# Attention on one Trainium2 core: the next step's scores issued one head per quarter of a step

## The chip, the cores and the metric

The kernel runs on one NeuronCore of one Trainium2 chip. The metric is the device time of one execution in microseconds (us): 3027.41 before the change, the median of three runs (3024.32 to 3032.85).

Names used below: PE is TensorE, DVE is VectorE, ACT is ScalarE, POOL is GpSimd, and SP is the engine that here issues the loads and stores. PSUM is the memory that PE writes; one of its eight banks holds 512 float32 values in each of the 128 partitions.

## What is computed

A block of mixture-of-experts, attention, mixture-of-experts, each with a residual:

```python
x = x + 0.5 * ffn(layernorm(x))      # 8 experts, one per token, capacity 1024
x = x + attention(layernorm(x))
x = x + 0.5 * ffn(layernorm(x))
```

with x of 8 batches x 1024 tokens x 256, float32. The change concerns the attention alone, which has 16 heads of 16 columns:

```python
q, k, v = heads(Wq, bq), heads(Wk, bk), heads(Wv, bv)
q, k = rope(q), rope(k)
att = einsum('bhqd,bhkd->bhqk', q, k) / sqrt(16)      # causal
att = softmax(where(causal, att, -1e10))
y = einsum('bhqk,bhkd->bhqd', att, v)
return y @ Wp.T + bp
```

## The kernel before, in words

The program is a row of blocks: routing, experts, attention, routing (with attention's last projection), experts. In the profile the attention takes about 815 to 2230 us of the span.

**Groups and steps.** Attention works through 32 *groups*; a group is four heads of one batch. A group has 12 *steps* (`STEPS`, L50): in a step the four heads' scores are computed of one block of 128 keys against up to 512 queries (half a batch). Steps 0 to 3 belong to the first half of the queries, steps 4 to 11 to the second. A step on the diagonal has fewer columns (steps 1, 2, 3 and 5, 6, 7 have 128, 256 and 384) and a second matmul that adds the mask (L1440). So four kinds of work run in each step:

- *Scores* (`scores`, L1428): per head one matmul, and on the diagonal the mask matmul, into one of `BANKS` = 3 PSUM banks, `score_ps`. A head's score waits on `exp_done` until the exponential that read that bank three heads earlier is done.
- *Exponentials* (`exponentials`, L1318) on ACT, one per head, from `score_ps` to `probs`. ACT also copies the finished half `o_ps` (L1316), and splits the rotated q and k of a later pair of token tiles into parts (`first_parts` L1306, `second_parts` L1311) in steps 1, 3 and 5.
- *Times V* (`times_v`, L1443): four heads side by side in the array, from `probs` to `o_ps`. It waits until all four exponentials of its own step are done, and in steps 0 and 4 for ACT's copy of `o_ps`.
- The *ring* (`ring`, L1415 on PE, L1179 on DVE): for the group after, PE computes scores again, queries by keys, into one of three banks `max_ps`, and DVE takes each row's maximum. 48 such matmuls per group, and two transposes of the finished maxima (`FIRST` and `SECOND`, L1419), are dealt out over the 12 steps and within a step over its four *quarters* c = 0 to 3 (`share`, L113). A ring matmul waits until DVE has read its bank three places earlier. The maxima are subtracted inside the score matmul: they go as three more rows into q. For that DVE splits them into three bfloat16 parts (`split_peaks`, L1208), PE transposes these, DVE copies them to `peak_t`, and SP writes them to memory and reads them back into q (`move_peaks`, L982 to L990). The scores of steps 0 and 4 wait for this second transfer (`peak_loaded`, L1433).

**Preparation.** In between, each group prepares two more token tiles, six groups ahead (`piece`, L1502): PE transposes rotated q and k in steps 0 and 3, normalized x in step 5, and multiplies by the weights in steps 6, 8 and 10; all go through the one bank `prep_ps`, which DVE (`leave` L1173, `xt_low` L1153, `add_bias_qk` L1159) and ACT read. POOL rotates (`rope`, L1053) and makes the third part (`third_parts`, L1078). SP then stores the pair (`store_pair`, L954), loads q, k and v of the group after next (`load_group`, L967: 13 transfers), and only then does it move the next group's maxima of the first half (`move_peaks(..., 0)`). These waits and transfers stand in one queue, that of SP. From group 27 on nothing is left to prepare.

**The order within a step.** It is written out by hand in `body` of the PE program (L1488). Before the change a quarter is: piece, then in quarters 0 and 1 the scores of two heads of the step after, then in quarter 2 times V of this step, then the ring's share. The scores of the next group's step 0 are issued in step 11. That point, the first score matmul of a group, is called the *group's start* below.

Of the kernel before, what the change touches and what calls it, by code (L numbers as in the profile page):

```python
# [22 lines left out]
P = 128  # L23
# [15 lines left out]
GH = 4  # L39
# [9 lines left out]
BANKS = 3  # L49
STEPS = [(0, j) for j in (0, 3, 2, 1)] + [(1, j) for j in (0, 7, 6, 5, 4, 1, 2, 3)]  # L50
NS = len(STEPS)
HALF = S // 2
# [763 lines left out]
def attention_block(nc, sh, dr):  # L816
# [6 lines left out]
    with ExitStack() as ctx:  # L823
# [9 lines left out]
        q = [sb(f"q{k}", [ROWS_M, GH, S], BF16) for k in range(SLOTS)]  # L833
        kk = [sb(f"k{k}", [ROWS_M, GH, S], BF16) for k in range(SLOTS)]
# [70 lines left out]
        score_ready = sem("score_ready")  # L905
# [29 lines left out]
        def slot_round(g, k, ahead):  # L935

            if isinstance(g, int):
                return (g + ahead) % SLOTS, (g + ahead) // SLOTS
            return (k + ahead) % SLOTS, g // SLOTS + (k + ahead) // SLOTS
# [423 lines left out]
        def _(pe):  # L1363
# [61 lines left out]
                te.matmul(max_ps[bank(u, r)][:, 0:w], q[u][0:ROWS, h, i * P:(i + 1) * P], kk[u][0:ROWS, h, k0:k0 + w],  # L1425
                          start=True, stop=True).then_inc(max_ready, 1)

            def scores(g, u, t, pr):  # L1428

                c0, w, diagonal = columns(STEPS[t])  # L1430
                hf, j = STEPS[t]
                if t in FIRST_STEP.values() and pr == 0:
                    pe.wait_ge(peak_loaded[hf], 16 * (g + 1))  # L1433
                for h in range(2 * pr, 2 * pr + 2):
                    pe.wait_ge(exp_done, GH * (NS * g + t) + h + 1)
                    out = score_ps[(GH * t + h) % BANKS]
                    last = te.matmul(out[:, 0:w], kk[u][:, h, j * P:(j + 1) * P],  # L1437
                                     q[u][:, h, hf * HALF + c0:hf * HALF + c0 + w], start=True, stop=not diagonal)
                    if diagonal:
                        last = te.matmul(out[:, 0:P], sh.ident_bf[:], hide_bf[:], start=False, stop=True)  # L1440
                    last.then_inc(score_ready, 1)

            def times_v(g, u, t):  # L1443
                c0, w, _ = columns(STEPS[t])
# [37 lines left out]
            pe.wait_ge(qkv_loaded[1], 16 * LOADS)  # L1482
            for r in RING_STEPS[NS - 1]:
                ring(1, 1, r)
            for pr in range(2):
                scores(0, 0, 0, pr)

            def body(g, k, more, prepare, finish):  # L1488
                n = g + LEAD
                for t in range(NS):  # L1490
# [29 lines left out]
                                product_v(n, s)  # L1520

                    for c in range(SHARES):
                        piece(c)
                        if c < 2:
                            if t + 1 < NS:
                                scores(g, k, t + 1, c)
                            elif more:
                                scores(g + 1, slot_round(g, k, 1)[0], 0, c)
                        if c == 2:
                            times_v(g, k, t)  # L1530
                        places(c)
# [101 lines left out]
```

## Time and profile before

| | before |
|---|---|
| median of three runs | 3027.41 us (3024.32 to 3032.85) |
| the profiled execution | 3024.25 us, with a span of 3022.4 us |
| PE busy | 2263.0 us (75% of the span), 14405 matmuls |
| weight loads busy | 1441.9 us (48%) |
| DVE busy | 1717.5 us (57%) |
| ACT busy | 1193.7 us (39%) |
| POOL busy | 961.9 us (32%) |
| mean granted TensorE clock | 0.898 of full speed |
| scores, 1536 matmuls (L1437) | 448.7 us, 337 ns each |
| mask, 1024 matmuls (L1440) | 219.4 us, 226 ns each |
| exponentials, 1536 (L1324) | 648.4 us, 495 ns each |

How to read it: busy is the time in which at least one instruction of the engine was under way. PE's matmuls overlap: a row lists the time from a matmul's start to its modelled end, and the next may start before that end. So two starts, one after the other, tell better what a matmul costs PE than its duration does, and an idle time listed before a matmul is shorter than the wait was. The clock is the share of full speed that the chip granted to TensorE: 1.00 is 2.4 GHz, 0.5 is 1.2 GHz, and a value between is a mean over a stretch in which both occurred. In a timeline the columns are start, duration (both us), engine, line, operation, written tile and read tiles, shape and count, and in brackets the engine's idle time before it with what ended it; "issue" there means nothing that the profile can name on another engine, such as a DMA.

### The profile page before, as it was taken

What the parts mean: (1) busy time and instruction counts of PE and PEld (TensorE: products, weight loads), DVE (VectorE), ACT (ScalarE), POOL (GpSimd) and SP (SyncE); (2) the same over time, 40 slices, a digit from 0 to 9 for tenths busy, and PEclk for the clock granted to TensorE, in tenths of its full rate; (3) what the DMA queues carried; (4) which work ended last, traced back from release to release, by engine and by line L of the source; (5) the groups of instructions that cost most, each with busy time, mean ns of one, the idle gap of its engine ahead of it and who ended that gap; (6) DMA issues with size and microseconds to landing.
All of it is one profiled execution on the core that took longest, in us unless ns stands there. A gap on an engine that the chain in (4) does not pass through costs nothing. (4 is left out here: it accounts for less than half of the span.)

```text
span 3022.4 us, 43677 instructions
## 1 busy us (share of the span) xinstructions
PE 2263.0 (75%) x14405; PEld 1441.9 (48%) x14405; DVE 1717.5 (57%) x5075; ACT 1193.7 (39%) x2498; POOL 961.9 (32%) x1308
## 2 busy tenths in 40 slices
PE   2704999974488888888888888888945550499997
PEld 2704888863333333333333333332315550488887
DVE  3503555534277776777677676776726660355553
ACT  1202444431135555555555555555631120244443
POOL 1173444324513232222222223320013427344442
PEclk9999999995579999999999999999976665699999
DMA  8026323202534455446355445534322202622320
GB/s 339 0 99 209 100 72 100 70 22 84 122 64 92 90 103 98 95 88 117 78 100 103 89 80 99 99 75 87 68 80 90 83 1 95 213 99 69 99 73 20
DMA packets 227444, 284.52 MB, mean 94 GB/s; under 512 B 21303, under 2 KB 171704, under 8 KB 225184
## 3 DMA queue, kind: packets, MB, share of 16 engines
q1 hardware_dynamic: 214944, 248.68, 33.3%
q0 software_dynamic: 12288, 33.21, 3.1%
q8 instruction: 110, 1.80, 0.3%
q14 instruction: 102, 0.84, 0.1%
HBM read 154.78 MB, written 127.66 MB: 93 GB/s over the span
## 5 line engine op out<-in xcount | busy, mean ns | idle before, releaser
L1324 ACT ACTIVATE at_probs<-at_score_ps 128x512 f32<-128x512 f32 (+3 forms) x1536 | 648.4, 495 | 521.6 <-PE at_score_ps L1440 379.0
L1203 DVE CUSTOM_DVE_ANT_0 at_junk<-at_max_ps,at_causal 128x128 f32<-128x128 f32 (+3 forms) x1024 | 490.5, 485 | 233.2 <-PE at_max_ps L1425 227.7
L1437 PE MATMUL at_score_ps<-at_q,at_k 99*128 99x512 bf16 (+3 forms) x1536 | 448.7, 337 | 89.9 <-ACT at_probs L1324 50.1
L1425 PE MATMUL at_max_ps<-at_k,at_q 96*128 96x512 bf16 (+3 forms) x1536 | 455.5, 342 | 9.9 <-DVE at_peak L1206 6.3
L1206 DVE TENSOR_REDUCE at_peak<-at_max_ps 128x1 f32<-128x512 f32 x512 | 352.1, 688 | 152.1 <-PE at_max_ps L1425 150.2
L728 DVE TENSOR_TENSOR f_hid_lo<-f_hid,f_hid_hi 128x512 fp32r<-128x512 f32 x256 | 177.5, 693 | 311.2 <-ACT f_hid_hi L752 310.8
L1450 PE MATMUL at_o_ps<-at_probs,at_v 128*32 128x512 f32 (+3 forms) x3072 | 340.9, 517 | 0.1
L790 PE MATMUL f_y_ps<-f_w_hi,f_hid_hi 128*128 128x256 f32 x1024 | 292.9, 286 | 40.4 <-DVE f_xe L709 28.9
L749 ACT ACTIVATE f_hid<-f_hid_ps 128x512 f32<-128x512 f32 x256 | 153.1, 598 | 418.1 <-PE f_hid_ps L775 393.0
L1425 PEld LDWEIGHTS at_max_ps<-at_k,at_q 96*128 96x128 bf16 x1536 | 129.6, 99 | 348.8 <-DVE at_peak L1203 144.7
L790 PE MATMUL f_y_ps<-f_w_hi,f_hid_lo 128*128 128x256 f32 x1024 | 291.5, 285 | 0.0
L790 PE MATMUL f_y_ps<-f_w_lo,f_hid_hi 128*128 128x256 f32 x1024 | 290.2, 283 | 0.0
L1437 PEld LDWEIGHTS at_score_ps<-at_q,at_k 99*128 99x128 bf16 x1536 | 143.7, 99 | 262.5 <-ACT at_probs L1324 152.9
L1064 POOL TENSOR_TENSOR at_by_cos<-at_qk,at_cos 128x512 f32<-128x512 f32 x64 | 81.4, 1272 | 534.2 <-DVE at_qk L1162 534.2
L653 POOL TENSOR_SCALAR f_xn<-f_xe 128x256 f32<-128x256 f32 x128 | 175.1, 1375 | 214.0 <-PE f_xt_ps L763 134.7
L790 PEld LDWEIGHTS f_y_ps<-f_w_hi,f_hid_hi 128*128 128x128 f32 x1024 | 194.3, 190 | 63.4 <-issue 41.2
L1440 PE MATMUL at_score_ps<-at_hide_bf,ident_bf 128*128 128x128 bf16 x1024 | 219.4, 226 | 0.0
L763 PE MATMUL f_xt_ps<-ident,f_xn 128*128 128x128 f32 x256 | 39.9, 282 | 217.1 <-POOL f_xn L653 217.1
L790 PEld LDWEIGHTS f_y_ps<-f_w_lo,f_hid_hi 128*128 128x128 f32 x1024 | 194.2, 190 | 9.0
L790 PEld LDWEIGHTS f_y_ps<-f_w_hi,f_hid_lo 128*128 128x128 f32 x1024 | 194.1, 190 | 0.0
L1080 POOL TENSOR_TENSOR at_part<-at_rest,at_part 128x512 bf16<-128x512 f32 x64 | 74.0, 1156 | 341.9 <-ACT at_part L1311 341.9
L775 PE MATMUL f_hid_ps<-f_xt_hi,f_w_hi 128*128 128x512 f32 x512 | 167.8, 409 | 14.9 <-DVE f_w_lo L691 14.9
(140 smaller groups left out, 3843.6 us busy)
## 6 DMA issues: line engine op xcount, KB each, us to landing
f_w_raw<-in_w SPq DMA_DIRECT2D x32, 1024.0 KB, 7.5
qk<-at_part SPq DMA_DIRECT2D x96, 256.0 KB, 2.9
at_q<-qk SPq DMA_DIRECT2D x192, 128.0 KB, 4.9
at_k<-qk SPq DMA_DIRECT2D x192, 128.0 KB, 7.7
expert_in<-zeros SPq DMA_DIRECT2D x16, 1040.0 KB, 25.6
f_xe<-expert_in SPq DMA_DIRECT2D x32, 520.0 KB, 3.7
v_rows<-at_v_out SPq DMA_DIRECT2D x64, 256.0 KB, 3.6
at_v<-v_rows SPq DMA_DIRECT2D x32, 512.0 KB, 9.6
```

What stands on the lines that cost most here:

```text
L653: last = nc.gpsimd.tensor_scalar(xn[:, t, :], x[:, t, 0:C], x[:, t, MEAN:MEAN + 1], x[:, t, RSTD:RSTD + 1], ALU.subtract, ALU.mult)
L728: v.tensor_tensor(hid_lo[f % NHID][:], hid[f % NHID][:], hid_hi[f % NHID][:].bitcast(F32), ALU.subtract).then_inc(hid_lo_ready, 1)
L749: nc.scalar.activation(hid[f % NHID][:], hid_ps[f % 2][:], ACT.Gelu_apprx_tanh).then_inc(hid_ready, 1)
L775: last = nc.tensor.matmul(hid_ps[f % 2][:], w[ws][:, cc, f * P:(f + 1) * P], x[b % 2][:, cc, :], start=(i == 0), stop=(i == 3 * CC - 1))
L790: last = nc.tensor.matmul(y_ps[t][:], a[m][:, rows], w[ws][:, f, :], start=(f == 0 and i == 0), stop=(f == FC - 1 and i == 2))
L1203: v.tensor_tensor_reduce(junk[bank(k, r)][:, 0:w], src, causal[:, HALF - w:HALF], 1.0, LEAST, ALU.add, ALU.max, out).then_inc(max_used, 1)
L1206: v.tensor_reduce(out, src, AX.X, ALU.max).then_inc(max_used, 1)
L1324: a.activation(probs[t % 2][:, h, c0:c0 + w], score_ps[(GH * t + h) % BANKS][:, 0:w], ACT.Exp, scale=float(SCALE)).then_inc(exp_done, 1)
L1425: te.matmul(max_ps[bank(u, r)][:, 0:w], q[u][0:ROWS, h, i * P:(i + 1) * P], kk[u][0:ROWS, h, k0:k0 + w], start=True, stop=True).then_inc(m ...
L1437: last = te.matmul(out[:, 0:w], kk[u][:, h, j * P:(j + 1) * P], q[u][:, h, hf * HALF + c0:hf * HALF + c0 + w], start=True, stop=not diagonal)
L1440: last = te.matmul(out[:, 0:P], sh.ident_bf[:], hide_bf[:], start=False, stop=True)
L1450: last = te.matmul(o_ps[h * VW:(h + 1) * VW, c0:c0 + w], vv[u][:, j, h, :], probs[t % 2][:, h, c0:c0 + w], start=(t == FIRST_STEP[hf]), st ...
```

## The change

`scores` now takes one head instead of a pair. In each of the four quarters of a step it is called first, ahead of piece, times V and the ring's share. The four heads' scores of the step after so stand at the start of quarters 0, 1, 2 and 3, where two stood in each of quarters 0 and 1, behind the piece.

```diff
-            def scores(g, u, t, pr):
+            def scores(g, u, t, h):
...
-                if t in FIRST_STEP.values() and pr == 0:
+                if t in FIRST_STEP.values() and h == 0:
                     pe.wait_ge(peak_loaded[hf], 16 * (g + 1))
-                for h in range(2 * pr, 2 * pr + 2):
-                    pe.wait_ge(exp_done, GH * (NS * g + t) + h + 1)
...
+                pe.wait_ge(exp_done, GH * (NS * g + t) + h + 1)
...
                     for c in range(SHARES):
+                        if t + 1 < NS:
+                            scores(g, k, t + 1, c)
+                        elif more:
+                            scores(g + 1, slot_round(g, k, 1)[0], 0, c)
                         piece(c)
-                        if c < 2:
-                            if t + 1 < NS:
-                                scores(g, k, t + 1, c)
-                            elif more:
-                                scores(g + 1, slot_round(g, k, 1)[0], 0, c)
                         if c == 2:
                             times_v(g, k, t)
                         places(c)
```

The instructions are the same on every engine, and on DVE, ACT, POOL and SP their order is the same too. Only PE's order moves. (In the changed kernel L1437, L1440 and L1450 are L1436, L1439 and L1449.)

The first place is step 2 of a group on PE: the scores of step 3 (384 columns, with mask) and times V of step 2 (256 columns). Before:

```order
L1437 MATMUL at_score_ps<-at_q,at_k 128x384
L1440 MATMUL at_score_ps<-at_hide_bf,ident_bf 128x128
L1437 MATMUL at_score_ps<-at_q,at_k 128x384
L1440 MATMUL at_score_ps<-at_hide_bf,ident_bf 128x128
L1437 MATMUL at_score_ps<-at_q,at_k 128x384
L1440 MATMUL at_score_ps<-at_hide_bf,ident_bf 128x128
L1437 MATMUL at_score_ps<-at_q,at_k 128x384
L1440 MATMUL at_score_ps<-at_hide_bf,ident_bf 128x128
L1425 MATMUL at_max_ps<-at_k,at_q 128x512
L1450 MATMUL at_o_ps<-at_probs,at_v 32x256 x4
L1425 MATMUL at_max_ps<-at_k,at_q 128x512
```

Changed:

```order
L1436 MATMUL at_score_ps<-at_q,at_k 128x384
L1439 MATMUL at_score_ps<-at_hide_bf,ident_bf 128x128
L1436 MATMUL at_score_ps<-at_q,at_k 128x384
L1439 MATMUL at_score_ps<-at_hide_bf,ident_bf 128x128
L1425 MATMUL at_max_ps<-at_k,at_q 128x512
L1436 MATMUL at_score_ps<-at_q,at_k 128x384
L1439 MATMUL at_score_ps<-at_hide_bf,ident_bf 128x128
L1449 MATMUL at_o_ps<-at_probs,at_v 32x256 x4
L1436 MATMUL at_score_ps<-at_q,at_k 128x384
L1439 MATMUL at_score_ps<-at_hide_bf,ident_bf 128x128
L1425 MATMUL at_max_ps<-at_k,at_q 128x512
```

The first ring matmul moved ahead of the third score, and times V ahead of the fourth.

The second place is step 11 on PE, from the first mask matmul after the group's start to the transpose of the second half's maxima. Before:

```order
L1440 MATMUL at_score_ps<-at_hide_bf,ident_bf 128x128
L1437 MATMUL at_score_ps<-at_q,at_k 128x512
L1440 MATMUL at_score_ps<-at_hide_bf,ident_bf 128x128
L1425 MATMUL at_max_ps<-at_k,at_q 128x128 x2
L1437 MATMUL at_score_ps<-at_q,at_k 128x512
L1440 MATMUL at_score_ps<-at_hide_bf,ident_bf 128x128
L1437 MATMUL at_score_ps<-at_q,at_k 128x512
L1440 MATMUL at_score_ps<-at_hide_bf,ident_bf 128x128
L1425 MATMUL at_max_ps<-at_k,at_q 128x128 x2
L1450 MATMUL at_o_ps<-at_probs,at_v 32x512 x4
L1425 MATMUL at_max_ps<-at_k,at_q 128x256 x3
L1419 MATMUL at_max_ps<-ident_bf,at_peak_part 48x128
```

Changed:

```order
L1425 MATMUL at_max_ps<-at_k,at_q 128x128 x2
L1436 MATMUL at_score_ps<-at_q,at_k 128x512
L1439 MATMUL at_score_ps<-at_hide_bf,ident_bf 128x128
L1425 MATMUL at_max_ps<-at_k,at_q 128x128 x2
L1436 MATMUL at_score_ps<-at_q,at_k 128x512
L1439 MATMUL at_score_ps<-at_hide_bf,ident_bf 128x128
L1449 MATMUL at_o_ps<-at_probs,at_v 32x512 x4
L1425 MATMUL at_max_ps<-at_k,at_q 128x256 x2
L1436 MATMUL at_score_ps<-at_q,at_k 128x512
L1439 MATMUL at_score_ps<-at_hide_bf,ident_bf 128x128
L1425 MATMUL at_max_ps<-at_k,at_q 128x256
L1419 MATMUL at_max_ps<-ident_bf,at_peak_part 48x128
```

Each pair of ring matmuls stands one score earlier, and the first two 256-column ones now come after three scores instead of four.

The third place is step 3 on PE, where the scores are those of step 4 and the transposes of rotated q and k (L1410) are the piece. Before:

```order
L1410 MATMUL at_prep_ps<-ident,at_rot 128x128 x2
L1437 MATMUL at_score_ps<-at_q,at_k 128x512 x2
L1410 MATMUL at_prep_ps<-ident,at_rot 128x128 x2
L1437 MATMUL at_score_ps<-at_q,at_k 128x512 x2
L1425 MATMUL at_max_ps<-at_k,at_q 128x512
L1450 MATMUL at_o_ps<-at_probs,at_v 32x384 x4
L1425 MATMUL at_max_ps<-at_k,at_q 128x512
```

Changed:

```order
L1436 MATMUL at_score_ps<-at_q,at_k 128x512
L1410 MATMUL at_prep_ps<-ident,at_rot 128x128 x2
L1436 MATMUL at_score_ps<-at_q,at_k 128x512
L1410 MATMUL at_prep_ps<-ident,at_rot 128x128 x2
L1425 MATMUL at_max_ps<-at_k,at_q 128x512
L1436 MATMUL at_score_ps<-at_q,at_k 128x512
L1449 MATMUL at_o_ps<-at_probs,at_v 32x384 x4
L1436 MATMUL at_score_ps<-at_q,at_k 128x512
L1425 MATMUL at_max_ps<-at_k,at_q 128x512
```

The second transposes end after two scores in both orders; the ring matmul and times V stand ahead of the fourth score.

## Rows read from the trace of the kernel before

**Rows 1.** Busy time by stretch; one whole group, steady state.

```profile
core 0: us, PE busy (x) PEld busy (x) DVE busy (x) ACT busy (x) POOL busy (x), PEclk, DMA share, GB/s
1305.30:1349.74 44.44, 38.92 (x264) 16.80 (x263) 31.97 (x109) 24.00 (x55) 12.98 (x22) 0.96 0.45 91
```

**Rows 2.** Who waited for whom, PE, 945 to 2017 us (24 groups): total, times, longest.

```profile
PE at_score_ps L1437 <- ACT at_probs L1324: 37.3, 97, 1.0
PE at_max_ps L1419 <- DVE at_peak_part L1227: 31.2, 24, 1.8
PE at_score_ps L1437 <- issue: 23.9, 18, 2.5
```

**Rows 3.** Timeline around one group's start, SP and PE.

```profile
1323.18 1.52 SPq L960 DMA_DIRECT2D qk<-at_part  x3
...
1335.56 0.36 SPq L986 DMA_DIRECT2D peaks<-at_peak_t  x1
1344.56 0.72 SPq L989 DMA_DIRECT2D at_q<-peaks  x1
...
1346.94 0.38 PE L1437 MATMUL at_score_ps<-at_q,at_k 99*128 99x512 bf16 x1 [0.49 <-issue]
```

**Rows 4.** Busy time of first halves, group's start to store issue; columns of rows 1.

```profile
902.33:923.99 21.66, 18.67 (x138) 7.98 (x138) 15.10 (x65) 13.43 (x35) 6.61 (x8) 0.92 0.07 26
...
1302.49:1323.18 20.69, 17.25 (x138) 7.77 (x138) 15.36 (x67) 13.41 (x35) 6.61 (x7) 1.00 0.07 27
...
1702.73:1726.97 24.24, 21.34 (x146) 9.34 (x146) 15.19 (x66) 13.90 (x35) 6.79 (x8) 0.80 0.06 24
...
sum 552.02, PE 466.59 PEld 207.18 DVE 405.67 ACT 349.27 POOL 171.66; mean PE 17.95 PEld 7.97 DVE 15.60 ACT 13.43 POOL 6.60
```

**Rows 5.** The same for 25 second halves, store issue to next group's start.

```profile
1057.58:1079.81 22.23, 20.07 (x127) 8.47 (x126) 15.97 (x42) 10.55 (x22) 6.37 (x15) 1.00 0.84 156
...
1411.41:1435.61 24.20, 20.08 (x127) 8.49 (x126) 16.65 (x43) 10.54 (x22) 6.36 (x15) 1.00 0.82 143
...
sum 583.10, PE 518.17 PEld 219.06 DVE 402.75 ACT 263.77 POOL 156.75; mean PE 20.73 PEld 8.76 DVE 16.11 ACT 10.55 POOL 6.27
```

**Rows 6.** Timeline of PE, steps 1 and 3 of one group.

```profile
1310.34 0.22 PE L1440 MATMUL at_score_ps<-at_hide_bf,ident_bf 128*128 128x128 bf16 x1
1310.75 0.28 PE L1437 MATMUL at_score_ps<-at_q,at_k 99*128 99x256 bf16 x1 [0.20 <-ACT at_probs L1324]
1310.87 0.22 PE L1440 MATMUL at_score_ps<-at_hide_bf,ident_bf 128*128 128x128 bf16 x1
1310.93 0.33 PE L1425 MATMUL at_max_ps<-at_k,at_q 96*128 96x384 bf16 x1
...
1314.96 0.38 PE L1437 MATMUL at_score_ps<-at_q,at_k 99*128 99x512 bf16 x1
...
1316.30 0.39 PE L1437 MATMUL at_score_ps<-at_q,at_k 99*128 99x512 bf16 x1 [0.96 <-ACT at_probs L1324]
1316.53 0.38 PE L1425 MATMUL at_max_ps<-at_k,at_q 96*128 96x512 bf16 x1
```

**Rows 7.** Timeline of ACT, steps 3 and 4, the same group.

```profile
1315.16 0.58 ACT L1306 CAST at_part<-at_prep_ps 128x512 bf16<-128x512 f32 x1 [0.77 <-PE at_prep_ps L1410]
1315.64 2.07 ACT L1324 ACTIVATE at_probs<-at_score_ps 128x512 f32<-128x512 f32 x4
```

**Rows 8.** Timeline of PE, DVE and POOL, step 11.

```profile
1305.65 1.27 POOL L1064 TENSOR_TENSOR at_by_cos<-at_qk,at_cos 128x512 f32<-128x512 f32 x1 [11.89 <-DVE at_qk L1162]
...
1305.98 0.96 DVE L1227 TENSOR_TENSOR at_peak_part<-at_peak_rest,at_peak_part 128x16 bf16<-128x16 f32 x1
...
1307.09 0.22 PE L1419 MATMUL at_max_ps<-ident_bf,at_peak_part 128*48 128x128 bf16 x1 [1.43 <-DVE at_peak_part L1227]
```

**Rows 9.** Timeline of ACT and POOL, step 5.

```profile
1321.11 0.62 ACT L1311 CAST at_part<-at_rest 128x512 bf16<-128x512 f32 x1 [1.93 <-DVE at_rest L1176]
...
1321.80 1.15 POOL L1080 TENSOR_TENSOR at_part<-at_rest,at_part 128x512 bf16<-128x512 f32 x1 [6.17 <-ACT at_part L1311]
```

**Rows 10.** Who waited for whom, PE, 2069 to 2210 us (last groups).

```profile
PE at_score_ps L1437 <- ACT at_probs L1324: 5.3, 22, 0.4
```

More of the change, by code:

```diff
@@ L1426, in ring @@
                           start=True, stop=True).then_inc(max_ready, 1)
-            def scores(g, u, t, pr):
+            def scores(g, u, t, h):
                 c0, w, diagonal = columns(STEPS[t])
                 hf, j = STEPS[t]
-                if t in FIRST_STEP.values() and pr == 0:
+                if t in FIRST_STEP.values() and h == 0:
                     pe.wait_ge(peak_loaded[hf], 16 * (g + 1))
-                for h in range(2 * pr, 2 * pr + 2):
-                    pe.wait_ge(exp_done, GH * (NS * g + t) + h + 1)
[L1436 to L1441, printed above, removed]
+                pe.wait_ge(exp_done, GH * (NS * g + t) + h + 1)
+                out = score_ps[(GH * t + h) % BANKS]
+                last = te.matmul(out[:, 0:w], kk[u][:, h, j * P:(j + 1) * P],
+                                 q[u][:, h, hf * HALF + c0:hf * HALF + c0 + w], start=True, stop=not diagonal)
+                if diagonal:
+                    last = te.matmul(out[:, 0:P], sh.ident_bf[:], hide_bf[:], start=False, stop=True)
+                last.then_inc(score_ready, 1)
             def times_v(g, u, t):
@@ L1484, in _ @@
                 ring(1, 1, r)
-            for pr in range(2):
-                scores(0, 0, 0, pr)
+            for h in range(GH):
+                scores(0, 0, 0, h)
             def body(g, k, more, prepare, finish):
```

## The prediction, made before the changed kernel ran

> **What bounds the kernel now.** I read four views. First the busy time by stretch: in a steady group [rows 1] PE is busy 38.92 of 44.44 us, DVE 31.97, ACT 24.00. No engine is full, so what counts is who waits for whom. Second, the waits of PE over 24 groups [rows 2]: the scores wait for exponentials (37.3 us, 97 times, so four times a group), the transpose of the second half's maxima for DVE (31.2 us, once a group), and the scores wait 18 times for something that is on no engine (23.9 us). Third, the timeline around a group's start [rows 3]: that last wait ends 2.38 us after SP issued the read of the maxima into q at 1344.56. Their write had been issued at 1335.56 and waited 9 us among the 13 loads, which stand behind the store at 1323.18. So one chain is SP's: store, loads, maxima, group's start.
>
> Fourth, I cut each group in two: the first half from the group's start to the issue of the store, the second from there to the next start. Second halves [rows 5] last 22.2 to 24.2 us, on average 583.10 / 25 = 23.3, though PE needs only 20.1 us of each at full clock, and the DMA share is over 0.8. In 18 of 24 groups, then, the second half is as long as its transfers. First halves [rows 4] move almost nothing (DMA share 0.07). They last 20.69 us at full clock, and longer where the clock was lower: 21.66 at 0.92, 24.24 at 0.80. Their end is set by engines: DVE frees `prep_ps` (L1176), ACT splits at 1321.11, POOL at 1321.80 [rows 9], and the store follows.
>
> The reader is to see this: **what PE saves in a first half brings the store, and with it the whole period, forward. What it saves in a second half only makes the wait at the group's start longer.**
>
> **The change part by part.** No instruction is added or removed; each of 32 groups has its 48 scores in another place on PE.
>
> *The fourth head's score.* It needs the bank of the first head of its own step, so that exponential must be over; the other three wait for those of the step before. Where all four are issued within quarters 0 and 1, PE stands still for it. A mask matmul that is not held up is followed 0.06 us later by the next (1310.87, 1310.93); the one before the fourth head by 0.41 (1310.34, 1310.75), a wait of 0.35 us of which the row shows 0.20 as idle [rows 6]. The same sum gives 0.35 in step 2 and 0.13 in step 0. In step 3 it is 1316.30 less 1314.96, less 0.23 for a 512-column score: 1.1 us, because ACT first does its cast at 1315.16 and begins the exponentials at 1315.64 [rows 6, 7]. Now times V stands between. In step 1 it has 128 columns and is the shortest, in step 3 384. I walked the steps forward with these rows: the first exponential is over before times V is, except in step 3, where PE would reach the fourth score at about the time that the exponential begun at 1315.64 ends (about 0.6 us later: four take 2.07, overlapping), and some 0.2 us of waiting remain. The cast itself comes no earlier by the new order, since the second transposes stand behind two scores as before. First halves gain 0.13 + 0.35 + 0.35 + 0.9 = **1.75 us**. Bounds: nothing, if the next exponential is late in the same measure, and 1.95.
>
> *The maxima in step 11.* PE stands idle 1.43 us until DVE has made the last part [rows 8]. That instruction took 0.96 us though it has 16 columns, and ended as POOL's product of 1305.65 ended (1305.98 + 0.96 = 1306.94; 1305.65 + 1.27 = 1306.92). POOL's product waits for DVE's bias addition (L1162), which stands behind ring places issued in quarters 0 and 1. These now stand one score (0.28 us with its mask) or two earlier, and the wait of the fourth score in between is gone (0.24). So the bias addition, POOL's product and the last part all come about 0.6 us earlier. Gain **0.6 us**, between 0 and the whole 1.43 that would be free if DVE came ahead of POOL.
>
> *What follows in the first half.* Steps 4 and 5 hang on DVE: from the last ring place of step 3 to the release of `prep_ps` it works without a pause. It is moved forward as a whole by what PE gained until then. Two waits that PE newly meets in step 4 (for the second and third exponential, and for ACT's copy of `o_ps`) stand beside this DVE work, which is the longer; I cost them at nothing. If they were longer than DVE's work, up to 0.5 us a group would be lost. No engine becomes full: DVE's 15.4 us of a first half would fill 15.4 of 18.3.
>
> Sum of a first half: 1.75 + 0.6 = 2.35 us. There are 27 with such a store: **63 us**.
>
> *Second halves.* Similar waits go there too (steps 5, 7 and 9, and the earlier rings in step 5), about 1.3 us by the same arithmetic. Six or seven of 25 second halves ended without a wait at the start and have 0.3 to 0.5 us of room before their transfers bind: **3 us**. The rest only lengthens the wait at the group's start.
>
> *The last groups* have no store and few transfers, and are bound by PE and ACT. Scores wait 5.3 us in 22 places as idle time [rows 10], and each is 0.15 longer as in rows 6: 8.6 us. I take nearly all: **8 us**.
>
> *The clock.* After the longest waits at a group's start the granted clock is lower. Eight of 26 first halves are at 0.92 or less; all 26 sum to 552.02 us [rows 4], 14.1 over 26 x 20.69, so 1.7 us for each of the eight. Of the waits at a start, 2.5 us at most [rows 2], the seven longest are the ones followed by it. With 1.3 us added to each wait some 18 are as long as those seven are now, and I count 18 of 26 first halves in place of eight: ten more, **17 us lost**. Bounds: none more (0), all 26 (31).
>
> The Trainium skill, "TensorE: Matmul & The Clock Gate", section "HAM oscillation — how this bites in real kernels", says that a wait for a DMA between batches of matmuls takes the clock back to half, so that each batch starts cold, every time. This speaks against the change. The rows agree for the long waits and not for the short ones; by that rule the loss would be the upper bound, 31 us.
>
> Total: 63 + 3 + 8 - 17 = 57 us off the profiled execution's 3024.25, that is 2967. The median of the runs is 3.2 above that execution: **2970 us**.
>
> **The rivals.**
>
> *Every group starts cold.* For it: waits at the start grow in every group. Against: 1.3 us more leaves many below the length of the seven. 14 us slower than the forecast: 2984.
>
> *The wait only moves.* The three banks `score_ps` are as few as before. If the fourth exponential, asked for later, is late for quarter 2 of the next step, only the gain in step 11 is left: 27 x 0.6 = 16, so 3011. For it: the exponentials of 512 columns start every half microsecond, and a step of few columns has little PE work from quarter 3 to the next quarter 2. Against: ACT is busy 13.4 of 20.69 us in first halves [rows 4]. The Trainium skill, "Perfetto Trace Analysis", section "Optimization Strategy" (under "Identifying Performance Opportunities"), says that a gap that repeats can mean too few buffers in PSUM; by that reading an order alone gives little, and this rival's time is what it would give.
>
> *Second halves gain too*, if the transfers run faster once the engines do: 1.3 us in 25 halves, 32 us, and no more cold starts: 2921. Against: 150 GB/s whatever PE does [rows 5].
>
> *Slower.* In the new order the fourth score stands behind times V, and times V of the next step needs its exponential. If PE then waits a whole exponential (0.6 us) in each of a first half's six steps, that is 3.6 us against 2.35 gained: 1.25 x 27 = 34 us slower, 3061. It decides from 0.4 us a step on. Against: between a fourth score and the next times V stand three more scores and two or three ring matmuls, in wide steps over 1 us of PE work.
>
> *No change*: first halves gain, and the transfers' half grows by as much. Nothing in rows 5 speaks for it.
>
> **How the numbers follow.** Forecast 0.55 (2970); every group cold 0.14 (2984); the wait moves 0.14 (3011, or part of it); second halves too 0.09 (2921); slower 0.05 (3061); no change 0.03. A difference of 0.3%, 9 us, is about what the measurement can tell. Faster by more: 0.55 + 0.14 + 0.14 + 0.09 = 0.92. Slower by more: 0.05. Within: 0.03. For the range: the bounds of the forecast's own terms reach from full gain without more cold starts (1.95 + 0.8 per first half, 74 + 3 + 8 = 85 off, 2942) to half the gain of first halves with the middle clock loss (31 + 3 + 8 - 17 = 25 off, 3002). I take 2938 to 3004, which leaves out the third rival's end, part of the second and the last two.
>
> **What would show it.** Right: from step 0 to 3 no idle before the fourth head's score but some 0.2 us in step 3; the transpose of the maxima waits about 0.8 us, not 1.43; first halves at full clock of about 18.3 us; second halves as long as before (23.3); more and longer waits at the group's start; more first halves below full clock. Wrong: first halves of 20 us or more with waits of scores for exponentials in quarter 0 to 2; second halves clearly longer or shorter than 23.3; a period of 44 us as now.

## The result: 2.7% faster, and the profile after

| | before | changed |
|---|---|---|
| median of four runs | 3029.58 us (3024.32 to 3032.85) | 2945.26 us (2938.67 to 2954.99) |
| ratio, 95% interval | | 0.9732 [0.9714, 0.9751] |
| the profiled execution | 3024.25 us | 2954.99 us |
| PE / DVE / ACT busy, share of span | 75 / 57 / 39% | 75 / 58 / 41% |

The change saves 84 us by the medians. The profiled execution of the changed kernel is the longest of its four, that of before is shorter than all of its four, so the two traces show less: 3022.4 - 2953.2 = 69.2 us of span. The forecast was 57 off one profiled execution, 2970 us, in a range of 2938 to 3004. Time and sign were right; of the size, 57 us was forecast where the profiled executions show 69 and the medians 84. Among all executions named below one stands apart, 5038.8 us in the run "fourth score alone", whose median is therefore taken over its other three.

The page of the changed kernel begins:

```profile
span 2953.2 us, 43675 instructions
...
PE 2219.3 (75%) x14403; PEld 1436.2 (49%) x14405; DVE 1702.0 (58%) x5075; ACT 1222.7 (41%) x2498; POOL 962.5 (33%) x1308
```

The waits of PE, changed kernel, 937 to 1956 us (25 groups), beside [rows 2]:

```profile
PE at_score_ps L1436 <- issue: 64.6, 24, 4.4
...
PE at_max_ps L1419 <- DVE at_peak_part L1227: 14.9, 20, 1.1
PE at_max_ps L1425 <- DVE at_peak L1203: 12.2, 42, 0.5
```

The first line of [rows 2], 97 waits for exponentials, has no counterpart: there is none in this stretch. The wait for the last part of the maxima is halved (31.2 to 14.9 us). The wait at the group's start has nearly tripled, 23.9 to 64.6. That is the answer in three lines: one wait went, one was halved, and one took part of the room. The last line above is smaller: ring matmuls, which now stand earlier, wait for DVE 42 times in first halves, where before it was once (0.3 us). On the other hand, the preparation's transposes of x no longer wait for DVE's release of `prep_ps`, which before read

```profile
PE at_prep_ps L1371 <- DVE at_rest L1176: 8.4, 24, 0.4
```

The busy time by stretch of the changed kernel, first halves (columns as in [rows 1]); beside [rows 4]:

```profile
1101.46:1119.71 18.25, 16.96 (x145) 7.96 (x146) 15.26 (x66) 13.61 (x34) 6.61 (x7) 1.00 0.08 31
1144.59:1163.98 19.39, 18.45 (x145) 8.37 (x146) 15.16 (x66) 13.74 (x34) 6.61 (x7) 0.91 0.08 30
...
sum 497.76, PE 467.46 PEld 213.04 DVE 396.23 ACT 353.43 POOL 171.73; mean PE 17.98 PEld 8.19 DVE 15.24 ACT 13.59 POOL 6.61
```

and the second halves, here 26 where [rows 5] has 25 (the first one of before, 23.81 us, makes 606.9 of its 583.1):

```profile
1078.63:1101.46 22.83, 19.36 (x118) 8.37 (x117) 15.96 (x43) 11.30 (x22) 6.38 (x15) 1.00 0.84 151
...
sum 604.66, PE 504.78 PEld 217.81 DVE 414.33 ACT 293.59 POOL 163.36; mean PE 19.41 PEld 8.38 DVE 15.94 ACT 11.29 POOL 6.28
```

First halves took 552.0 us in all and now take 497.8: 54.3 less. Second halves took 606.9 and now take 604.7: 2.3 less, although PE is busy 20.70 - 19.41 = 1.3 us less in each on average, 0.74 of it at full clock (20.10 and 19.36). At full clock a first half is 18.25 us where it was 20.69.

Where the other 69.2 - 56.5 = 12.7 us came from: every 48th score matmul begins a group. The start of group 1 comes 5.9 us earlier (902.3 to 896.4), the stretch from group 27's start to group 31's is 9.0 us shorter (138.8 to 129.8), and what follows that is 1.2 us longer. Of the 5.9 us, 3.4 lie before group 0's start (857.22 to 853.84), ahead of any instruction whose place was changed; in the runs below with pairs prepared six ahead that start lies between 852.1 and 856.2 us, in either order. Group 0 itself gained 2.6 us (45.1 to 42.5). Its second half is the first of the 26 above, so 0.8 us stand in both counts.

The places themselves. Step 3 of a first half, timeline of PE in the changed kernel, beside [rows 6, 7]:

```profile
1112.94 0.85 PE L1449 MATMUL at_o_ps<-at_probs,at_v 128*32 128x384 f32 x8
1113.75 0.39 PE L1436 MATMUL at_score_ps<-at_q,at_k 99*128 99x512 bf16 x1
```

and of ACT in the same step:

```profile
1112.61 0.58 ACT L1306 CAST at_part<-at_prep_ps 128x512 bf16<-128x512 f32 x1
1113.09 2.07 ACT L1324 ACTIVATE at_probs<-at_score_ps 128x512 f32<-128x512 f32 x4
```

The fourth score at 1113.75 has no idle time before it: the exponential begun at 1113.09 ran beside times V and was over at 1113.70. Before, 1.1 us of standing still were here.

Step 11 of the same group, timeline of POOL, DVE and PE, beside [rows 8]; the group's start was 1101.46:

```profile
1104.00 1.26 POOL L1064 TENSOR_TENSOR at_by_cos<-at_qk,at_cos 128x512 f32<-128x512 f32 x1 [12.07 <-DVE at_qk L1162]
...
1104.75 0.54 DVE L1227 TENSOR_TENSOR at_peak_part<-at_peak_rest,at_peak_part 128x16 bf16<-128x16 f32 x1
...
1105.44 0.22 PE L1419 MATMUL at_max_ps<-ident_bf,at_peak_part 128*48 128x128 bf16 x1 [0.73 <-DVE at_peak_part L1227]
```

POOL's product starts 2.54 us after the group's start, where it was 3.16; PE's transpose follows at 3.98, where it was 4.60. DVE's 16-column instruction again ends when POOL's product ends (1105.29 and 1105.26).

SP's chain is as it was, 9 us from the write of the maxima to their read in [rows 3] and here, and the start comes 2.37 us after the read is issued. SP's queue in the changed kernel, before another start:

```profile
1133.15 0.36 SPq L986 DMA_DIRECT2D peaks<-at_peak_t  x1
1142.22 0.72 SPq L989 DMA_DIRECT2D at_q<-peaks  x1
```

and PE's first instruction at that start:

```profile
1144.59 0.40 PE L1436 MATMUL at_score_ps<-at_q,at_k 99*128 99x512 bf16 x1 [4.40 <-issue]
```

### The profile page after: what moved, and what is told of

The parts are those of the page before. It is cut to its first block and busy times, and to the rows that moved or that the text cites. A ratio compares the mean times of both kernels' runs of the same rounds, so it can differ in the third digit from the quotient of the medians.

```text
span 2953.2 us, 43675 instructions
## 1 busy us (share of the span) xinstructions
PE 2219.3 (75%) x14403; PEld 1436.2 (49%) x14405; DVE 1702.0 (58%) x5075; ACT 1222.7 (41%) x2498; POOL 962.5 (33%) x1308
## 5 line engine op out<-in xcount | busy, mean ns | idle before, releaser
L1324 ACT ACTIVATE at_probs<-at_score_ps 128x512 f32<-128x512 f32 (+3 forms) x1536 | 690.8, 498 | 512.3 <-PE at_score_ps L1439 371.4
L1436 PE MATMUL at_score_ps<-at_q,at_k 99*128 99x512 bf16 (+3 forms) x1536 | 503.7, 335 | 83.6 <-issue 79.7
L1425 PE MATMUL at_max_ps<-at_k,at_q 96*128 96x512 bf16 (+3 forms) x1536 | 489.4, 341 | 23.2 <-DVE at_peak L1203 14.9
L1449 PE MATMUL at_o_ps<-at_probs,at_v 128*32 128x512 f32 (+3 forms) x3072 | 342.5, 519 | 1.5 <-ACT at_o_out L1316 0.8
L1425 PEld LDWEIGHTS at_max_ps<-at_k,at_q 96*128 96x128 bf16 x1536 | 144.6, 99 | 378.0 <-DVE at_peak L1203 163.6
L1436 PEld LDWEIGHTS at_score_ps<-at_q,at_k 99*128 99x128 bf16 x1536 | 151.3, 99 | 202.1 <-issue 92.9
L1439 PE MATMUL at_score_ps<-at_hide_bf,ident_bf 128*128 128x128 bf16 x1024 | 227.3, 224 | 0.0
L790 PEld LDWEIGHTS f_y_ps<-f_w_hi,f_hid_hi 128*128 128x128 f32 x1024 | 194.3, 190 | 63.5 <-issue 41.7
L775 PE MATMUL f_hid_ps<-f_xt_hi,f_w_hi 128*128 128x512 f32 x512 | 167.5, 408 | 14.6 <-DVE f_w_lo L691 14.6
L700 DVE TENSOR_TENSOR f_xt_lo<-f_xt_ps,f_xt_hi 128x512 fp32r<-128x512 f32 x64 | 44.3, 692 | 229.7 <-ACT f_xt_hi L740 229.7
```

The source lines that it names most:

```text
L775: last = nc.tensor.matmul(hid_ps[f % 2][:], w[ws][:, cc, f * P:(f + 1) * P], x[b % 2][:, cc, :], start=(i == 0), stop=(i == 3 * CC - 1))
L790: last = nc.tensor.matmul(y_ps[t][:], a[m][:, rows], w[ws][:, f, :], start=(f == 0 and i == 0), stop=(f == FC - 1 and i == 2))
L1324: a.activation(probs[t % 2][:, h, c0:c0 + w], score_ps[(GH * t + h) % BANKS][:, 0:w], ACT.Exp, scale=float(SCALE)).then_inc(exp_done, 1)
L1449: last = te.matmul(o_ps[h * VW:(h + 1) * VW, c0:c0 + w], vv[u][:, j, h, :], probs[t % 2][:, h, c0:c0 + w], start=(t == FIRST_STEP[hf]), st ...
```

## The experiments

The theory (T): the gain is that of waits removed in first halves; second halves are as long as SP's transfers. Rivals: it comes from all twelve steps alike; or from the scores' place ahead of the pieces, not from the fourth one's place behind times V. Each run was compared with runs of the kernel before on the same chip; the medians of those were 3022.7 to 3033.0 us, so ratios compare better than times. The means are of the profiled executions: 26 halves in the runs with pairs six ahead, and for first halves 25 with pairs seven ahead. The kernel before has 21.23 and 23.34. With pairs seven ahead the last of the 26 second halves has nothing left to prepare (14.6 us in the new order, 15.6 in the old); without it the means are 20.52, 22.15 and 20.40 in the table's order. In the run with early maxima the store stands elsewhere, and the halves do not compare.

| run | median, us | ratio, 95% interval | first halves, mean | second halves, mean |
|---|---|---|---|---|
| changed kernel | 2945.3 | 0.9732 [0.9714, 0.9751] | 19.14 | 23.26 |
| new order in first halves only | 2948.5 | 0.9739 [0.9691, 0.9786] | 18.78 | 23.21 |
| new order in second halves only | 3033.2 | 1.0022 [0.9999, 1.0045] | 22.20 | 23.25 |
| fourth score alone | 2956.8 | 0.9757 [0.9693, 0.9821] | 19.44 | 23.23 |
| pairs ahead of pieces | 3044.3 | 1.0064 [1.0044, 1.0084] | 21.90 | 23.27 |
| new order in step 11 only | 3007.4 | 0.9935 [0.9918, 0.9951] | 20.82 | 23.41 |
| new order, early loads | 2894.8 | 0.9570 [0.9553, 0.9586] | 19.00 | 21.18 |
| old order, early loads | 2995.6 | 0.9903 [0.9886, 0.9919] | 20.95 | 22.61 |
| new order, early loads and maxima | 2900.8 | 0.9581 [0.9566, 0.9597] | | |
| new order, pairs seven ahead | 2872.6 | 0.9490 [0.9472, 0.9508] | 18.68 | 20.30 |
| old order, pairs seven ahead | 2980.2 | 0.9838 [0.9785, 0.9890] | 20.72 | 21.90 |
| changed kernel, POOL waits | 2944.8 | 0.9747 [0.9725, 0.9769] | 19.03 | 23.09 |
| new order, seven ahead, POOL waits | 2862.9 | 0.9463 [0.9447, 0.9478] | 18.36 | 20.18 |

### First halves alone, second halves alone

The quarter loop decides by step:

```diff
+NEW_STEPS = (11, 0, 1, 2, 3, 4)        # the other run: (5, 6, 7, 8, 9, 10)
...
                     for c in range(SHARES):
-                        if t + 1 < NS:
-                            scores(g, k, t + 1, c)
...
+                        heads([c] if t in NEW_STEPS else [])
                         piece(c)
+                        heads(range(2 * c, 2 * c + 2) if t not in NEW_STEPS and c < 2 else [])
```

> The new order in steps 11 and 0 to 4 alone, which feed the store; steps 5 to 10 keep the old one. If second halves are bounded by their transfers, nearly the whole gain stays: first halves of 18.25 us at full clock, second halves near 23.3, a time within 10 us of the changed kernel's 2945 (the last groups lose some 4 us, fewer first halves at low clock may give some back). If the gain came evenly from all twelve steps, half of it is left: about 2985.

> The new order in steps 5 to 10 alone. If second halves are bounded by their transfers: first halves stay at 20.69 us, second halves near 23.3, the wait at the group's start grows by 1 us or more, and the time is 3015 to 3030 (3 us from the groups that had no wait, 4 from the last ones, less what more low clock costs). If the gain came evenly from all twelve steps: about 2985.

Measured: 2948.5 and 3033.2 us, the second 3 above its range. The six steps that feed the store bring the whole gain (0.9739 against 0.9732); the other six bring none, or lose a little (the interval just includes no change). Waits of PE in the second run, new order in steps 5 to 10 only, 945 to 2030 us:

```profile
PE at_score_ps L1437 <- issue: 60.9, 22, 4.2
PE at_score_ps L1437 <- ACT at_probs L1325: 31.7, 68, 1.0
```

Its busy time by stretch: one first half, then the sums over 26 first and 26 second halves:

```profile
896.15:917.95 21.80, 19.06 (x145) 8.03 (x146) 15.55 (x66) 13.42 (x34) 6.60 (x7) 0.92 0.07 26
...
sum 577.29, PE 508.71 PEld 218.85 DVE 401.38 ACT 351.24 POOL 171.72; mean PE 19.57 PEld 8.42 DVE 15.44 ACT 13.51 POOL 6.60
...
sum 604.58, PE 506.07 PEld 218.33 DVE 413.68 ACT 293.51 POOL 163.65; mean PE 19.46 PEld 8.40 DVE 15.91 ACT 11.29 POOL 6.29
```

PE's work in second halves shrank here as in the changed kernel, yet these halves take 604.6 us (606.9 before), and the wait at the start went from 23.9 to 60.9 us. First halves, whose order is the old one, rose from 552.0 to 577.3 us: 39 us over 26 x 20.69 where it was 14. The row at 896.15 shows where: the same order, a granted clock of 0.92, and 1.1 us more than the 20.69 of a first half at full clock. Its start follows a wait:

```profile
896.15 0.38 PE L1437 MATMUL at_score_ps<-at_q,at_k 99*128 99x512 bf16 x1 [2.70 <-issue]
```

Of the 26 first halves 24 are like it, at 0.92 or less, where it was eight before. So time saved where a transfer is waited for was worth nothing here, and went with a lower clock behind the longer wait. In this profiled execution (3038.1 us) the lower clock took more than the 2.3 us that the second halves gained. Over all executions the loss is at the edge of what is measured.

### Which part of the order counts

First the fourth score alone, `heads(([0, 1], [2], [], [3])[c])` behind the piece:

> The old order, in which only the fourth head's score is moved, from quarter 1 to quarter 3, behind times V. If that score's wait is what the change removes, first halves keep the 1.75 us of it and part of the 0.6 in step 11: 18.5 to 19.2 us at full clock, and a time of 2950 to 2970. If it is the place of the other scores ahead of the pieces and one by one that counts, first halves stay above 20 us and the time above 3005.

Measured: 2956.8 us, first halves of 18.68 us at full clock. One row of this run:

```profile
895.43:914.11 18.68, 17.02 (x145) 7.96 (x146) 15.44 (x66) 13.28 (x34) 6.60 (x8) 1.00 0.08 31
```

Of the 2.44 us that a first half gained, 2.01 come with the fourth score's new place. The remaining 0.43 is left for the other three, which stand earlier and apart; that is a difference of two runs, not a run of its own.

Then the opposite: pairs as before, but ahead of the pieces.

```diff
+                        heads(range(2 * c, 2 * c + 2) if t != 3 and c < 2 else [])
                         piece(c)
+                        heads(range(2 * c, 2 * c + 2) if t == 3 and c < 2 else [])
```

> The scores stay in pairs in quarters 0 and 1 but stand ahead of the pieces, except in step 3, where the fourth score ahead of the second transposes would wait for an exponential that waits for these transposes. If the fourth score's wait is the matter, this keeps it: first halves of 20.4 to 20.9 us, time 3015 to 3035. If the place ahead of the pieces is the matter: below 2990.

Measured: 3044.3 us, slower by 0.6%. The waits of PE, 945 to 2030 us:

```profile
PE at_score_ps L1436 <- issue: 59.5, 25, 3.5
PE at_score_ps L1436 <- ACT at_probs L1324: 45.6, 98, 1.0
...
PE at_prep_ps L1380 <- DVE at_xt_lo L1155: 11.8, 24, 0.5
```

The 98 waits for exponentials are all there, and longer. What the order saves is a wait in step 6, of a second half (`at_xt_lo`, 25 to 29 us in the other runs of this length, here 11.8), and it comes back at the group's start with a lower clock behind it. That it was slower than its range of 3015 to 3035 I had not forecast; 24 of 26 first halves are at 0.92 or less here too, as with the new order in second halves only. The shortest first half at full clock was 20.66 us. So it is not the place ahead of the pieces.

### Step 11

`NEW_STEPS = (11,)`:

> The new order in step 11 alone. If the earlier ring places there bring DVE's last part of the maxima forward, first halves at full clock shorten by 0.6 us, from 20.69 to 20.1, and PE's wait for that part from 1.3 to about 0.8 us a group: 16 us in all, 3006 to 3015. If the whole gain of first halves comes from the fourth scores of steps 0 to 3, nothing: 3022.

Measured: 3007.4 us, 18 less than before; the shortest first half is 20.08 us, 0.61 less. Two rows, one whose start followed a wait and one whose start did not:

```profile
1165.33:1185.41 20.08, 17.25 (x138) 7.81 (x138) 14.83 (x65) 13.48 (x35) 6.61 (x7) 1.00 0.08 30
1208.50:1229.20 20.70, 17.59 (x139) 7.80 (x137) 16.03 (x68) 13.62 (x35) 6.61 (x7) 1.00 0.25 79
```

The 0.6 us appear only behind a wait at the start. The eight first halves whose start had none lasted 20.7 us or more, as before. Waits of PE, 945 to 2017 us:

```profile
PE at_score_ps L1437 <- ACT at_probs L1325: 37.9, 100, 1.0
...
PE at_max_ps L1420 <- DVE at_peak_part L1228: 16.5, 22, 1.1
```

The waits for exponentials stand, that for the maxima has halved, as forecast.

### Taking the transfers out of the second half

If transfers bound the second halves, moving them must free these. The loads of group g + 2 need the slot of group g - 1, free at the start of group g, and pairs already stored; in three groups of four these are stored a group earlier.

```diff
+                early = two_more and (g + 2) % NG != 0
+                if early:
+                    load_group(g + 2, slot_round(g, k, 2)[0])
                 store_o(g, 0)
                 if finish:
                     store_pair(g + LEAD - 1)
-                if two_more:
+                if two_more and not early:
                     load_group(g + 2, slot_round(g, k, 2)[0])
```

> The new order, and in three groups of four SP issues the 13 loads of the group after next at the beginning of its list, ahead of the store, in the first half, where the transfers have room (share 0.07). If transfers bound the second halves, the wait at the group's start goes in these groups, their second halves fall to 20.5 to 21.5 us, the others stay near 23.5: some 19 x 2.2 = 42 us, and fewer first halves at low clock, 10 more: about 2895. If something else bounds them (PE, DVE), second halves stay at 23.3 and the time at 2945.

> The old order with the same early loads. PE's own second half of 21.5 us (full clock) to 23.1 remains, so that 19 groups gain 1 us at most, and the low clock after long waits goes: 3000 to 3010. With the transfers out of the way the new order's gain is that of both halves, (2.4 + 1.3) x 27 + 8 = about 108 us, against 84 without early loads. If the second halves' waits were worth nothing in any case, the gain stays 84 or less.

Measured: 2894.8 and 2995.6 us. Two neighbouring second halves of the first of them, and the sum of 26:

```profile
914.39:934.73 20.34, 19.21 (x119) 8.43 (x118) 14.79 (x41) 10.73 (x22) 6.35 (x15) 1.00 0.30 89
953.70:977.40 23.70, 19.48 (x119) 8.37 (x117) 15.96 (x43) 11.41 (x22) 6.38 (x15) 1.00 0.78 146
...
sum 550.73, PE 501.49 PEld 219.17 DVE 391.46 ACT 282.08 POOL 163.05; mean PE 19.29 PEld 8.43 DVE 15.06 ACT 10.85 POOL 6.27
```

With the loads early (DMA share 0.30) a second half takes 20.34 us, with the loads in it (0.78) 23.70, and PE does the same work. This is the bound, shown by moving it. The old order gained only 30 us by it, since its own second half needs 21.5 us, and 23.0 or more where the clock is at 0.93, as in 14 of 26; the new order is now worth 101 us. I had expected 108, and the old order at 3000 or more.

A variant issues the maxima of the first half ahead of the store as well.

> As the run before with the new order, and the maxima of the first half are moved ahead of the store instead of behind the loads. In the one group of four whose loads must stay behind the store, the write of the maxima no longer waits some 9 us among the loads; the group's start then waits for the loads themselves, 1 us less: 6 x 1 = 6 us, so about 2888. Slower by up to 1 us a group where the store, now behind this round trip, holds something up.

Measured: 2900.8 us, 6 slower than without it instead of 6 faster. As expected, the start then waits for the loads themselves (PE's waits name `at_v<-v_rows`, 16.8 us in six places, where 19.5 us had no name). But six ring matmuls newly wait for DVE, 7.0 us in all, 6.1 of it in three places. In each of the three DVE stood still until the store of the previous pair had landed, because it writes the buffer `v_out` that this store reads:

```profile
1049.66 0.76 DVE L1172 TENSOR_TENSOR at_v_out<-at_prep_ps,at_bias 128x256 f32<-128x256 f32 x2 [2.58 <-DMA v_rows<-at_v_out]
```

It is the case that the expectation names last: the store, now behind the maxima's round trip, comes too late.

Last, all four groups of four. Preparing pairs seven groups ahead frees the fourth group's loads too.

```diff
-LEAD = 6
+LEAD = 7
...
-                early = two_more and (g + 2) % NG != 0
+                early = two_more
```

> New order, pairs prepared seven groups ahead instead of six, so that all four groups of four can take their loads early. If the 13 loads behind the store are what is left of the waits at a group's start, the six groups that still waited 3 to 4 us lose that wait and the low clock after it: 6 x 3.5 + 5 = 26 us off, less one more preparation ahead of the attention, 5 us: 2870 to 2880. If the waits have another cause: 2900.

> The old order with pairs seven ahead and all loads early, beside the same with the new order (2872.6). No transfer bounds a second half in either. If the waits that the new order removes are worth their full length once no transfer takes them back, the period is 20.7 + 21.5 us (full clock) or 23.1 (low clock in the second half) against 18.65 + 20.33, so 3.2 to 4.8 us x 26, and 8 in the last groups: 91 to 133 us, a time of 2964 to 3005. If they are worth only what they brought before, 84: below 2960.

Measured: 2872.6 us with the new order, 2980.2 with the old. Waits of PE with the new order, 945 to 1900 us, all of them:

```profile
PE at_prep_ps L1383 <- DVE at_xt_lo L1158: 23.7, 23, 1.0
PE at_max_ps L1422 <- DVE at_peak_part L1230: 18.6, 26, 1.0
PE at_max_ps L1428 <- DVE at_peak L1206: 9.2, 24, 0.5
PE at_max_ps L1428 <- DVE at_peak L1209: 0.2, 1, 0.2
PE at_score_ps L1439 <- DMA at_q<-peaks: 0.2, 1, 0.2
```

The wait at the start is gone, and with it the low clock behind it: from group 1 on no first half of this run is above 19 us; second halves are 20.3, but for three of 21.9 at a clock of 0.92. The new order is worth 107.6 us here against 84 in the kernel as it was (by the ratios 105 against 81). The difference, some 24 us, is what the transfers had been taking back: in the profiled executions first halves save 53 us here and 54 there, second halves 41.7 us here and 2.3 there. Of the 41.7, about 31 are the 1.2 us of each second half at full clock (21.53 to 20.33), and the rest is clock: ten second halves of the old order are at 0.93 and last 23.0 us or more.

A first half at full clock is mostly 18.65 us here, not 18.25 as in the changed kernel. As with step 11 alone, a part of what the new order gains shows only behind a wait at the start; without one it is 20.70 - 18.65 = 2.05 us.

### POOL and DVE in step 11

[Rows 8] and the row of the changed kernel suggest that DVE's last part waits for POOL's product. Here POOL waits for DVE instead:

```diff
                         if t == 11:
+                            pool.wait_ge(peak_ready, 2 * (g + 2))
                             rope(n, 1, 0)
```

> The changed kernel, in which POOL's first rotation product of step 11 waits until DVE has made the last part of the maxima. If this part ends late because POOL's product holds something that both need, DVE's instruction takes 0.17 us instead of 0.54, and the second transpose comes earlier: up to 0.5 us a group, 13 us, 2932 to 2940. If the length of that instruction has another cause, or if its wait is for the ring matmul ahead of it: unchanged, 2945, or up to 5 us slower by the later product.

> Both together: pairs seven groups ahead with all loads early, and POOL's wait. If the two are independent, the gain of POOL's wait (up to 13 us, or more now that second halves are no longer bounded by transfers only if it also shortens these) comes off the time of the seven-ahead kernel: 2860 to 2875. If the product's delay now matters: 2880 or more.

Measured: 2944.8 us on the changed kernel, no gain; 2862.9 on the kernel with pairs seven ahead, 9.7 less. In the first of the two the instruction and its successors read

```profile
1066.24 0.17 DVE L1228 TENSOR_TENSOR at_peak_part<-at_peak_rest,at_peak_part 128x16 bf16<-128x16 f32 x1
...
1066.55 0.22 PE L1420 MATMUL at_max_ps<-ident_bf,at_peak_part 128*48 128x128 bf16 x1 [0.36 <-DVE at_peak_part L1228]
```

and over its 64 occurrences, minimum, median and maximum in ns, it takes

```profile
L1228 DVE TENSOR_TENSOR at_peak_part<-at_peak_rest,at_peak_part x64: 168/170/176, 838.1 to 2124.8; 128x16 bf16<-128x16 f32 x64
```

where the maximum was 1043 before and 873 in the changed kernel. So it was held up by POOL's product: shown. The Trainium skill, "SBUF — State Buffer", section "SBUF: two separate sides", has the rule: a VectorE operation with both inputs in SBUF and a GpSimd operation that reads SBUF exclude each other, for the whole instruction; these rows agree. The shortest first half fell from 18.25 to 17.74 us. But the mean fell only from 19.14 to 19.03, since 20 of 26 first halves now had a clock of 0.92 or less, against 13. Half a microsecond a group was gained and nearly all given back. With the wait at the start gone, the same edit paid.

## Why the prediction was right, and where its sizes were off

**The chains.** That a first half moves the store and a second half only the wait held in every run that left the transfers where they were, and where they were moved second halves shortened, as this account demands.

**The fourth score.** Forecast 1.75 us a first half, with 0.2 left in step 3. None is left; moving that score alone brought 2.01. This includes what I had booked under step 11, where the same score now stands behind times V too; for steps 0 to 3 alone the two runs leave 2.44 - 0.61 = 1.83 of the whole new order.

**Step 11.** Forecast 0.6, measured 0.61 alone, but only behind a wait at the group's start. In the changed kernel every start has one, so the sum holds there: forecast 2.35, measured 20.69 - 18.25 = 2.44. With no wait at the start it is 2.05. That the gain depends on the wait I had not seen, and why it does stays open. The work on DVE in steps 4 and 5 was costed at nothing, and this sum leaves no room for a cost, although some ring matmuls now wait for DVE there.

**Second halves and last groups.** Forecast 3 and 8, measured 2.3 and 9.0. The 1.3 us that a second half could gain without transfers in its way was 1.2 (21.53 to 20.33).

**The clock: the term that was mis-sized.** Forecast: ten more first halves at a lower clock, 17 us lost. Measured: 23.3 us over 26 x 18.25, where it was 14.1, so 9 lost, and 13 such halves in place of 8. I had counted by the length of the wait at the start: whatever is as long as the seven longest of before, 1.76 us or more, brings the lower clock. The waits grew by more than I had said, from 1.0 to 2.7 us on average: 24 of 26 starts now follow a gap of 1.8 us or more, 23 of them more than 2. Yet half of the first halves are at full clock. The start at 1101.46 is one; its first instruction, in PE's timeline of the changed kernel, reads

```profile
1101.46 0.38 PE L1436 MATMUL at_score_ps<-at_q,at_k 99*128 99x512 bf16 x1 [2.34 <-issue]
```

and the first half behind it had clock 1.00. Length counts, but not by itself. In the changed kernel all eleven starts behind a gap of 2.87 us or more are followed by the lower clock, and of the 13 between 1.8 and 2.87 us only two.

The run with the new order in second halves only is the comparison that shows what I missed. Its waits at the start are as long as the changed kernel's, 68.8 us of idle time before 26 starts against 70.1, and the two kernels differ only in the order in steps 11 and 0 to 4. With the old order there 24 first halves are at 0.92 or less, with the new one 13; the loss is 39 us against 23. The other executions agree: the mean granted clock is 0.889 to 0.895 in all ten of the one and 0.898 to 0.901 in all four of the other. So the change, in the half where it gains, also kept first halves from the lower clock. My count of 18 fitted neither kernel, and that the term came out only 8 us too high is in part luck. Why the order matters to the clock, the runs do not show.

The Trainium skill, "TensorE: Matmul & The Clock Gate", section "HAM oscillation — how this bites in real kernels", tells of a kernel in which DMA waits of about 3 to 5 us left each batch cold. I had taken it for every wait, which gave the 31 us. For waits of that length the trace agrees: the nine starts with more than 3 us of idle time were all followed by the lower clock, of the 17 others four. The two runs with longer waits than before and nothing gained in first halves were the slowest: 3033.2 and 3044.3 us.

**What I left out.** The time up to group 1's start fell by 5.9 us; I had counted 2.4 there. Group 0 gave 2.6 of it, the other 3.4 lie before the change begins and vary from run to run. These terms make up the span: 54.3 + 1.5 (25 second halves) - 0.2 (group 26's) + 5.9 + 9.0 - 1.2 = 69.3 against 69.2. In the prediction's time for the rival of second halves, 2921 counts their 3 us twice; it should be 2924. The rest up to the 84 us of the medians lies between executions: the other three of the changed kernel took 2938.7 to 2945.4 us.

**The rivals.** *The wait only moves* is refuted. The Trainium skill, "Perfetto Trace Analysis", section "Optimization Strategy", says that a repeated gap can mean too few buffers in PSUM; here the gap went with three banks as before. *Second halves gain too* is refuted for the kernel as it was, and true once the loads are moved. *Slower* fell: in the steady groups PE's list of waits has neither a score nor times V waiting for an exponential. *No change* fell too: the transfers' half did not grow. *Every group starts cold* is true of 13 in 26.

## What to carry to other kernels

Before costing a removed wait, ask which chain ends the stretch it stands in. Here the same kind of wait was worth its full length in the half of a period that leads to a store, and nothing in the half that waits for transfers (one variant lost 0.6%). Nor is a wait that is left over free of effects: the same length of it went with the lower clock in 24 of 26 groups in one order of the work behind it, and in 13 of 26 in the other. Where a matmul must wait for a bank that its own step's first result frees, put the other engine-filling work of the step ahead of it; and once the engine waits for transfers instead, look at what stands ahead of them in their queue: moving 13 loads forward in SP's list, and preparing one group earlier, brought another 73 us.

## What the runs showed of the hardware

- Waits of about the same length at a group's start are followed by different granted clocks: 2.34 us idle and 1.00 in the changed kernel (start 1101.46), 2.33 and 2.05 us idle and 0.85 and 0.80 before (starts 1167.98 and 1702.73). With the old order in steps 11 and 0 to 4 the lower clock followed seven of seven gaps over 1.7 us (kernel before) and 24 of 25 (new order in second halves only), with the new order 13 of 24 (changed kernel). Why stays open.
- Saved time that turned into waiting cost clock: first halves of the old order rose from 21.23 to 22.20 us on average when only second halves were made shorter.
- A 16-column DVE instruction of 0.17 us took up to 1.04 us while POOL's product ran, and never more than 0.18 us when POOL was made to wait.
- The best version tried (new order, pairs seven ahead, all loads early, POOL waiting) takes 2862.9 us, 0.9463 [0.9447, 0.9478] of the kernel before.
